# Per-image totals on TensorE: four products on tiles of 32 columns behind the values' products, in place of one whole-array product behind the output projection

## The reference

```python
def _gn(v, G=16, eps=1e-5):
    B_, H_, W_, C_ = v.shape
    g = v.reshape(B_, H_, W_, G, C_ // G)
    m = jnp.mean(g, axis=(1, 2, 4), keepdims=True)
    s = jnp.var(g, axis=(1, 2, 4), keepdims=True)
    return ((g - m) / jnp.sqrt(s + eps)).reshape(v.shape)
...
q = xh @ Wq
k = xh @ Wk
v = xh @ Wv
...
sim = jnp.einsum('bmhid,bmhjd->bmhij', q2, k2) + pos_emb
attn = jax.nn.softmax(sim, axis=-1)
o = jnp.einsum('bmhij,bmhjd->bmhid', attn, v2)
o = o @ Wo + bo
...
x = x + _L0_conv_ref(_gn(x), L0_conv_Wq, L0_conv_Wk, L0_conv_Wv, L0_conv_Wo, L0_conv_bo, L0_conv_pos_emb, L0_conv_scale)
```

## Time and profile before

| | us |
|---|---|
| median of 3 runs | 3669.21 |
| lowest, highest | 3668.13, 3669.99 |
| the profiled execution | 3666.14 |
| its span in the trace | 3664.3 |
| PE busy | 3612.1 (99%) |
| DVE busy | 3032.6 (83%) |
| ACT busy | 2932.1 (80%) |
| POOL busy | 2053.3 (56%) |

### The profile page before, as it was taken

The page is one execution under the profiler, slowest core; times in us unless marked ns, Lnnn a source line. Parts: engine busy times, 40 slices in busy tenths (PEclk is TensorE's granted clock), DMA queues, the critical chain, the costliest instruction groups (busy, mean ns, idle before and its releaser), DMA issues.

```text
span 3664.3 us, 167562 instructions
## 1 busy us (share of the span) xinstructions
PE 3612.1 (99%) x67842; PEld 2624.8 (72%) x67842; DVE 3032.6 (83%) x5027; ACT 2932.1 (80%) x5377; POOL 2053.3 (56%) x3335
## 2 busy tenths in 40 slices
PE   6999999999999999999999999999999999999998
PEld 4777777777777777777777777777777777777776
DVE  6888888888888888888888888888888888888886
ACT  7887888888888888888888888887888888888874
POOL 5555555555555555555555555555555555555553
PEclk9999999999999999999999999999999999999999
DMA  4555555555555555555555555555555555555544
GB/s 101 141 139 144 146 144 135 146 144 144 135 144 144 144 135 146 143 145 135 143 147 142 137 144 145 144 136 145 144 146 134 145 144 145 134 146 144 145 124 120
DMA packets 255567, 513.67 MB, mean 140 GB/s; under 512 B 66352, under 2 KB 66800, under 8 KB 254992
## 3 DMA queue, kind: packets, MB, share of 16 engines
q1 hardware_dynamic: 253456, 504.35, 52.6%
q10 hardware_dynamic: 1536, 0.07, 0.0%
HBM read 118.31 MB, written 117.44 MB: 64 GB/s over the span
## 4 chain that ended last, share of the span: by engine, by line
PE 97%; ACT 1%; issue 1%; SPq 1%; DVE 0%; DMA 0%; POOL 0%; POOLq 0%; ACTq 0%
PE ps_out L343 20%; PE ps_q L343 18%; PE ps_k L343 18%; PE ps_v L343 16%; PE ps_o L386 14%; PE ps_s L374 11%; PE ps_tot L440 0%; ACT xn L505 0%; SPq L283 0%; SPq L311 0%; DMA x_sb<-in_x 0%; POOL xlo L781 0%; DMA p_bd<-pt_f 0%; POOL sc L770 0%; ACT xhi L528 0%
## 5 line engine op out<-in xcount | busy, mean ns | idle before, releaser
L770 POOL TENSOR_TENSOR sc<-sc,mx 128x512 f32<-128x512 f32 x512 | 537.5, 1050 | 870.9 <-DVE mx L703 870.8
L505 ACT ACTIVATE xn<-x_sb,norm_add,norm_mul 112x128 f32<-112x128 f32 x2048 | 1014.5, 598 | 1.8 <-issue 1.8
L791 POOL TENSOR_TENSOR sc<-sc,rs 128x512 f32<-128x512 f32 x512 | 537.3, 1049 | 424.9 <-DVE rs L723 424.8
L343 PE MATMUL ps_out<-ohi,wo_s 128*112 128x256 f16 x4096 | 720.6, 278 | 2.0 <-DVE x_sb L679 2.0
L547 ACT ACTIVATE sc<-sc 128x512 f32<-128x512 f32 x512 | 323.4, 632 | 446.2 <-POOL sc L770 446.2
L691 DVE TENSOR_TENSOR olo<-ps_o,ohi 128x512 f16<-128x512 f32 x512 | 354.1, 692 | 366.3 <-ACT ohi L562 356.7
L343 PE MATMUL ps_q<-xhi,wqk 112*128 112x512 f16 x2048 | 611.9, 380 | 5.9 <-issue 2.9
L343 PE MATMUL ps_k<-xhi,wqk 112*128 112x512 f16 x2048 | 610.2, 380 | 1.3 <-ACT k_cut L554 0.8
L386 PE MATMUL ps_o<-p_bd,v_sb 128*32 128x128 f32 x16384 | 553.4, 276 | 8.4 <-DMA p_bd<-pt_f 6.1
L343 PE MATMUL ps_v<-wv_s,xhi 112*128 112x224 f16 x4096 | 561.3, 260 | 0.0
L781 POOL TENSOR_TENSOR xlo<-xn,xhi 112x1024 f16<-112x1024 f32 x256 | 547.3, 2138 | 15.1 <-ACT xhi L528 15.1
(11 more groups left out here) (78 smaller groups left out, 5756.7 us busy)
## 6 DMA issues: line engine op xcount, KB each, us to landing
k_bd<-k_cut SPq DMA_DIRECT2D x1024, 128.0 KB
p_bd<-pt_f SPq DMA_DIRECT2D x2048, 64.0 KB, 2.5
x_sb<-in_x SPq DMA_DIRECT2D x256, 448.0 KB, 4.4
out_y<-x_sb SPq DMA_DIRECT2D x254, 448.0 KB, 3.5
out_y<-x_sb SPq DMA_DIRECT2D x8, 112.0 KB, 2.5
k_cut<-in_L_conv_Wq SPq DMA_DIRECT2D x2, 98.0 KB
k_cut<-in_L_conv_Wk SPq DMA_DIRECT2D x2, 98.0 KB
k_cut<-in_L_conv_Wv SPq DMA_DIRECT2D x2, 98.0 KB
```

What stands on the lines that cost most here:

```text
L343: last = nc.tensor.matmul(dst, w_parts(a, ch), x_parts(c, ch), start=(n == 0), stop=(n == 3 * chunks - 1))
L505: nc.scalar.activation(xn[:, b % 2, :, c4, :, :, nw].rearrange("p r c q -> p q r c"), x_sb[:, b % XBUFS].rearrange("p ch (nh r w) -> p (ch ...
L770: nc.gpsimd.tensor_tensor(rows, rows, mx[:, t % 2].unsqueeze(2).broadcast_to(by_row), ALU.subtract).then_inc(shifted, 1)
L791: nc.gpsimd.tensor_tensor(rows, rows, rs[:, t % 2].unsqueeze(2).broadcast_to(by_row), ALU.mult).then_inc(probs, 1)
```

## The change

The block that makes the totals moves up in TensorE's step: from behind the output projection to behind the values' products, ahead of the output projection. With it, the single product of 112 x 112 ones by 112 x 32 becomes four, on columns 0 to 31, 32 to 63, 64 to 95 and 96 to 111, each writing its own partitions of `ps_tot`. The last of the four signals `totals`. The waits are the same two, now one output projection earlier. The other engines' programs are unchanged.

```diff
                     weigh_values(g).then_inc(pv_done, 1)
+
+                b = {-TOT_LEAD + 8: None, -TOT_LEAD + 9: 2}.get(t, image_at(t, TOT_LEAD))
+                if b is not None:
+                    per_image(pe, joined, b, i)
+                    wait(pe, stats, STAT_OPS * (b - 1) + 1, i, STAT_OPS * XBUFS)
+
+                    for col in range(0, CP, 32):
+                        cols = slice(col, min(col + 32, CP))
+                        last = nc.tensor.matmul(ps_tot[cols, :], ones[0:CP, cols], both[:, b % 2], start=True, stop=True)
+                    last.then_inc(totals, 1)
                 g = t - OUT_LAG
                 if is_step(g):
...
                     last.then_inc(projected, 1)
-
-                b = {-TOT_LEAD + 8: None, -TOT_LEAD + 9: 2}.get(t, image_at(t, TOT_LEAD))
-                if b is not None:
-                    per_image(pe, joined, b, i)
-                    wait(pe, stats, STAT_OPS * (b - 1) + 1, i, STAT_OPS * XBUFS)
-                    nc.tensor.matmul(ps_tot[0:CP, :], ones[0:CP, 0:CP], both[:, b % 2],
-                                     start=True, stop=True).then_inc(totals, 1)
```

## The result

The changed kernel is slower: **3694.65 us**, the median of 6 runs (3689.51 to 3697.20), against 3668.67 us (3665.74 to 3670.54) for the kernel before in the same comparison. The ratio is 1.007, with a 95% interval from 1.0059 to 1.008, so 26 us were lost where a gain of 2 us had been forecast. The profiled execution of the changed kernel took 3689.5 us, with a span of 3687.7 us and a mean granted clock of 0.999, as before.

The account below looks back on a forecast made before the run. The ring of ACT, DVE and POOL bounds, PE within 0.4%. PE's 9.0 us go into waiting; the ring's 2.1 us less makes 3666.1 into 3664.0, plus 3.1 for the median, 3667 us; own range 3664 to 3671, overall 3660 to 3675.

Parts of the forecast that it names:

- Elsewhere: Effects outside the products and their wait: totals reach DVE 1.3 us sooner without gain; only PE's queue is moved past.
- the ring: Chain through ACT, DVE and POOL from `ohi` to the next `ohi`, said to set the pace at 169.05 us per 24 steps.
- the new wait is paid in each image: Rival: PE waits for `joined` at all 128 images, 0.25 us each, giving 3692 us; each or half of images, chance 0.08.
- Four products cost 0.06 us: On PE, four tiled products replace one of 0.13 us, saving 0.07 us an image, 9.0 us in all.
- A floor of 25 ns: Skill's minimum matmul start-to-start time on PE: eight would take 0.20 us, 9.0 us more in all; rejected for the trace.
- The ring sets the pace and swallows PE's gain: ACT, DVE and POOL are slower than PE by 0.3 to 0.7 us per 24 steps; PE's 9.0 us go into waiting.
- The wait for `both` limits itself: On PE ahead of the totals: a late image moves PE back against the ring; afterwards some 0.1 us an image.
- (1): Sign on PE: `ps_tot` adds 0.06 us between `ps_o` and `ps_out`; an undisturbed step with totals is 0.07 us shorter.
- (2): Sign on ACT: `ohi` starts 24 steps apart lie at 168.9 to 169.1 us; exponential waits for POOL in some 500 steps.
- (3): Sign on PE: it waits for `both` in some tens of images, 0.05 to 0.3 us each.
- (4): Sign on POOL: `both` is never done more than about 1.1 us behind the start of `ps_o`, before up to 1.24.
- The lateness of 0.25 us: Average price of PE's wait for `joined` in the rival paying it at each image: 128 x 0.25 = 32 us.

Follow-up runs that it names:

- the sixth: Changed kernel with 28 short products ahead of the loop and ACT copying `ohi` ahead of the bias additions: 3651.66 us, ratio 0.9949 to 0.9977.
- The twelfth: Changed kernel without padding, with ACT copying `ohi` ahead of the bias additions: 3678.95 us, ratio 1.0028 to 1.0058 to the kernel before.
- The second experiment: Kernel before with its one whole-array product moved ahead of the output projection: 3668.41 us, ratio 1.0003 to 1.0022.
- the first: Kernel before with the four products in the old place behind the output projection: 3716.59 us, ratio 1.0128 to 1.0162.
- the third: Changed kernel with 28 short products (112 PE instructions) ahead of the loop: 3663.87 us, ratio 0.9989 to 1.0008 to the kernel before.
- the tenth: Changed kernel with 36 short products ahead of the loop, loop's end at 59: ratio 1.0011 to 1.0034 to the kernel before.
- The fifth: Kernel before with ACT copying `ohi` ahead of the two bias additions, which shortens the ring: 3657.79 us against 3665.85, ratio 0.997 to 0.9989.
- the fourth experiment: Kernel before with 36 short products (144 instructions) ahead of the loop, totals unchanged: 3772.19 us, ratio 1.0276 to 1.031.
- the seventh: Changed kernel with 16 short products ahead of the loop, loop's end at 235: ratio 1.0111 to 1.0151 to the kernel before.
- the eighth: Changed kernel with 44 short products ahead of the loop, loop's end at 91: ratio 1.0126 to 1.0166 to the kernel before.

## Why the prediction was wrong, step by step

**The step that failed** is the one headed "Elsewhere": the prediction followed what the change moves in time and asked of PE's queue only what is passed in it. It had no term for the 144 instructions that the change adds on PE, 72 of them inside a hardware loop, and so **none for the jump back**. The profile of before had a trace of it, which I didn't use: PE's row of waits for issue ahead of `ps_q`, 2.9 us in 5 waits, and the gap of 0.21 us at 304.06. They show that the jump was already only just hidden, since 1.1 to 1.2 us of a jump is hidden by queued matmuls and the jump took 0.44 to 1.77 us. No row of before shows what another place would cost, so the size couldn't have been read; that a loop whose code grows has an unknown, one-sided risk at each of its 19 jumps could.

Nearly the whole loss is accounted for by that term. The ends of 192 steps in the changed kernel:

```profile
990.48 0.58 ACT L565 ACTIVATE ohi<-ps_o 128x512 f16<-128x512 f32 x1
...
2353.19 0.58 ACT L565 ACTIVATE ohi<-ps_o 128x512 f16<-128x512 f32 x1
```

That is (2353.19 - 990.48) / 8 = 170.34 us per 24 steps, against 169.05 before: 1.29 us in each of 20 passes is 26 us. PE's own work is now 24 x 6.99 + 6 x 0.062 = 168.1, with 0.3 us that PE shows beyond it wherever it is the bound (168.35 in the sixth), and the stall adds 1.76 a jump: 170.1. The last 0.2 us I put down to the ring, which is argued and not shown by a run: after each stall PE is late against the ring, with `both` done well over 1 us ahead of need at the first image; at the fifth PE has caught up, begins to wait for `both`, and goes at the ring's pace again until the next jump. The twelfth, with the shorter ring, lacks this part: 169.94.

**The rivals.** The measured time falls on one of them, "the new wait is paid in each image", whose number was 3692. The mechanism isn't that one. The second experiment has the new wait and no loss, the first has the loss and no new wait, and the third has both the four products and the wait and takes 3664 us. That its number is near the measured one is luck.

**What held**, now that the stall can be taken out (the third experiment):
- *Four products cost 0.06 us.* Measured 0.062 in the sixth and the tenth, the medians of step lengths with and without totals (7.050 against 6.988), and 0.129 before for the one product where 0.13 was read. PE's own step with totals is 0.067 us shorter; 0.07 was predicted. With the waits for `both` in it the difference is 0.111 in the changed kernel and 0.148 in the third experiment. A row without a wait, in the changed kernel:

```profile
1669.83 1.08 PE L386 MATMUL ps_o<-p_bd,v_sb 128*32 128x128 f32 x32
1670.73 0.25 PE L433 MATMUL ps_tot<-both,ones 112*32 112x32 f32 x8
1670.90 0.43 PE L343 MATMUL ps_out<-ohi,wo_s 128*112 128x256 f16 x2
```

From `ps_o` to `ps_out` it is 1.07 us here, against 1.01 in the earlier trace rows.
- *A floor of 25 ns doesn't hold here.* By the rule of the Trainium skill in "TensorE: Matmul & The Clock Gate" the eight would have taken 0.20 us; they add 0.062, as the rows had said.
- *The ring sets the pace and swallows PE's gain.* In the third experiment

```profile
985.42 0.57 ACT L567 ACTIVATE ohi<-ps_o 128x512 f16<-128x512 f32 x1
...
2336.40 0.57 ACT L567 ACTIVATE ohi<-ps_o 128x512 f16<-128x512 f32 x1
```

give 168.87 us per 24 steps; with an interval of 0.9989 to 1.0008, nothing of the 9 us of PE's work is seen in the time. The fifth and the sixth show the order of the two bounds by shortening the ring.
- *The wait for `both` limits itself.* In the third experiment:

```profile
1657.80 1.08 PE L386 MATMUL ps_o<-p_bd,v_sb 128*32 128x128 f32 x32
...
1658.64 0.25 POOL L743 TENSOR_TENSOR both<-part 112x32 f32<-112x32 f32 x1 [1.42 <-DVE part L672]
```
```profile
1659.03 0.26 PE L433 MATMUL ps_tot<-both,ones 112*32 112x32 f32 x8
1659.22 0.43 PE L343 MATMUL ps_out<-ohi,wo_s 128*112 128x256 f16 x2
```

`both` ends 1.09 us behind the start of `ps_o`, and `ps_out` begins at 1.42 in place of the 1.07 without a wait. Over the 120 images of the loop PE pays some 11 us like this, the 0.1 us an image of the prediction, and in the changed kernel, where the stall keeps it late, 4.9 us.

**The four signs.** (1), 0.06 and 0.07 us, was right. (2), `ohi` at 168.9 to 169.1 per 24 steps, is right without the stall (168.87) and wrong in the changed kernel (170.34), where the exponential waits for POOL 486 times. (3), waits in some tens of images of 0.05 to 0.3 us, was right for the changed kernel, with 41 of 0.02 to 0.28 us; in the third there are some 100, up to 0.47. (4) was right: `both` ends at most 1.03 us behind the start of `ps_o` in the changed kernel and 1.12 in the third.

Two slips in the working moved nothing. The lateness of 0.25 us is said to come from four images, but the earlier trace rows has the end of `both` for three, 0.31 us on the average; and 0.20 us for the four products gives 3672 us by the working's own terms, not 3673.

So the forecast of 3667 was about right for the change as a piece of work (no change within 0.1% in the third experiment), and wrong for the change as a program.

## What to carry to other kernels

Before an edit that adds or removes instructions on an engine inside a hardware loop is priced, look at that engine's "issue" waits at the loop's starts and at the packet count of the instruction queue, and look again after it: one more packet per pass, here 573 in place of 554, went with a jump back that waits for its code, 0.8 to 3.0 us of PE each time in these kernels. Where an edit of a loop gives a result that its own terms don't explain, run it again with a few dozen idle instructions ahead of the loop; that takes the place of the code out of the comparison, and here it turned 0.7% slower into no change. And where the busiest engine is at 99%, find out whether a ring of the others keeps the same pace: only with the ring shortened did the change pay, 3651.66 us against 3657.79.

## What the hardware did that I had not expected

- The jump back of one and the same loop takes 0.36 to 3.56 us in the mean, by where the loop's end lies modulo 256 instructions: short at 11, 27 and 59, long at 91, 171 and 235. In each kernel with long jumps the queue moved 18 to 20 packets of code more, one a pass. A count of the blocks that a pass touches fits all of them and stays to be tested.
- At 171 and 235, but not in every kernel at these places, a second stall of up to 2.0 us follows some 3 us later, ahead of `ps_v`. The two kernels that have it 19 times stop at the same point of the code modulo 256, 17 and 25 instructions behind the loop's start, which looks like a block's border right behind the jump's target; that it is the cause wasn't tried.
- With the two stalls of the fourth experiment (2.2 and 2.0 us at most) the granted clock was half for 3.4 to 6.8 us, 0.985 over the whole span; after the single stalls of the changed kernel, up to 2 us, it stayed at 0.999 over the span, as after the two shorter ones of the seventh at 0.998. After the single stalls of the eighth, up to 2.8 us, it was half for 3.4 us at 4 of the 19 jumps, 0.996 over the span.
- Tiled products between whole-array products cost 0.159 us a time more than one whole-array product there; the same four behind other tiled products cost 0.062 us in all.
